# Transformer tower on one core: tokens reordered on the chip, the first tile of batch 0 normalised at the hand-over

## The reference

```python
h = _L0_tok_ref(x, log_dt, log_w_real, w_imag, 512)      # h: 8 batches, 256 tokens, 512 channels
h = h + _L0_attn_ref(_layernorm(h), w_q, w_k, w_v, w_o)  # 16 heads of 128, 4 kv heads, causal, window 256, rope
h = h + _L0_ffn_ref(_layernorm(h), ...)                  # gate by best of 8 experts, rank-8 update
...
def _L0_tok_ref(C, log_dt, log_w_real, w_imag, L):
    dt = exp(log_dt)                                     # 256 tokens ("H"), 64 poles each
    w = -exp(log_w_real) + 1j * w_imag
    dtA = w * dt[:, None]
    Cm = (C[..., 0] + 1j * C[..., 1]) * (exp(dtA) - 1.0) / w
    return 2 * einsum('chn,hnl->chl', Cm, exp(dtA[:, :, None] * arange(L))).real
```

## Time and profile before

| | |
|---|---|
| median of 3 runs | 824.38 us (823.27, 824.38, 827.25) |
| profiled execution, its own time | 827.14 us |
| its span | 825.0 us |
| TensorE busy | 755.7 us, 92% |
| VectorE, ScalarE, GpSimd busy | 569.8, 455.9, 441.6 us |
| mean granted clock | 0.976 |

### The profile page before, as it was taken

One profiled execution on the slowest core, in us unless ns is written; L12 is line 12 of the kernel. 1 busy time (PEld: TensorE's weight loads), 2 busy tenths in 40 slices (PEclk: granted clock), 3 DMA queues, 4 the chain that ended last, 5 costly groups with the idle time before them and its releaser, 6 DMA issues.

```text
span 825.0 us, 19690 instructions
## 1 busy us (share of the span) xinstructions
PE 755.7 (92%) x6964; PEld 685.9 (83%) x6964; DVE 569.8 (69%) x1605; ACT 455.9 (55%) x1249; POOL 441.6 (54%) x656
## 2 busy tenths in 40 slices
PE   0377878899999999999999999999999999999997
PEld 0176667799999999999999999999999999988973
DVE  7999747777776655666666655656655777778876
ACT  6634326555555656555556565555756555455432
POOL 0497825544444747444447474444656555565532
PEclk9998988899999999999999999999999999999997
DMA  9023360100010102000001020000010000000002
GB/s 210 0 60 68 79 230 27 39 1 0 0 39 1 52 2 77 0 0 0 0 1 52 1 79 0 0 0 0 14 40 1 2 1 27 26 25 0 26 14 90
DMA packets 30503, 26.47 MB, mean 32 GB/s; under 512 B 22446, under 2 KB 22830, under 8 KB 30198
## 3 DMA queue, kind: packets, MB, share of 16 engines
q1 hardware_dynamic: 30310, 25.77, 11.0%
q10 hardware_dynamic: 144, 0.07, 0.0%
HBM read 17.44 MB, written 8.39 MB: 31 GB/s over the span
## 4 chain that ended last, share of the span: by engine, by line
PE 80%; DVE 8%; POOL 6%; issue 3%; ACT 1%; DMA 1%; DVEq 0%; SPq 0%; POOLq 0%; ACTq 0%
PE bank_quad L1270 17%; PE bank_quad L1272 17%; PE bank_quad L1271 17%; PE bank_pair L1272 4%; PE bank_pair L1270 4%; PE bank_pair L1271 4%; POOL w_lo L433 2%; PE bank_pair L1425 2%; PE bank_quad L1282 2%; PE bank_quad L1365 2%; PE bank L1435 2%; PE bank_pair L1435 1%; PE bank L1439 1%; DVE bank_pair L936 1%; POOL kq_lo L503 1%
## 5 line engine op out<-in xcount | busy, mean ns | idle before, releaser
L1270 PE MATMUL bank_quad<-xt_hi,w_hi 128*128 (+1 forms) x768 | 217.1, 283 | 0.8 <-POOL w_lo L433 0.8
L1272 PE MATMUL bank_quad<-xt_lo,w_hi 128*128 (+1 forms) x768 | 214.8, 280 | 0.0
L1271 PE MATMUL bank_quad<-xt_hi,w_lo 128*128 (+1 forms) x768 | 214.8, 280 | 0.0
L1024 DVE TENSOR_TENSOR kq<-bank_quad,cst 128x512 f32<-128x512 f32 (+1 forms) x96 | 57.9, 603 | 141.1 <-ACT swap L697 106.5
L499 POOL TENSOR_TENSOR swap<-swap,cst 128x512 f32<-128x512 f32 (+1 forms) x96 | 105.7, 1103 | 82.5 <-ACT swap L697 79.7
L1270 PEld LDWEIGHTS bank_quad<-xt_hi,w_hi 128*128 128x128 f32 x768 | 144.9, 189 | 2.8 <-POOL w_lo L433 1.4
L1272 PEld LDWEIGHTS bank_quad<-xt_lo,w_hi 128*128 128x128 f32 x768 | 144.8, 189 | 0.0
L1271 PEld LDWEIGHTS bank_quad<-xt_hi,w_lo 128*128 128x128 f32 x768 | 144.5, 188 | 0.0
L357 POOL TENSOR_TENSOR spare<-cst 1x1 f32<-1x1 f32 x85 | 16.8, 197 | 213.9 <-DVE rinv L1164 139.9
L737 ACT ACTIVATE sm<-sm,mx 128x128 f32<-128x128 f32 (+1 forms) x256 | 113.6, 445 | 21.7 <-DVE mx L1152 21.6
L696 ACT ACTIVATE swap<-bank_quad 64x512 f32<-64x512 f32 (+1 forms) x96 | 50.2, 523 | 125.8 <-PE bank_quad L1272 123.2
(11 more groups left out here) (309 smaller groups left out, 1877.6 us busy)
## 6 DMA issues: line engine op xcount, KB each, us to landing
mixed<-st SPq DMA_DIRECT2D x32, 128.0 KB, 2.0
out<-x SPq DMA_DIRECT2D x16, 256.0 KB, 2.0
raw<-in_w_qkv SPq DMA_DIRECT2D x8, 384.0 KB, 3.7
raw<-in_w_o SPq DMA_DIRECT2D x10, 256.0 KB, 2.7
x<-mixed SPq DMA_DIRECT2D x2, 1280.0 KB, 10.3
norm_mem<-in_w_qkv SPq DMA_DIRECT2D x6, 384.0 KB, 3.9
x<-mixed SPq DMA_DIRECT2D x3, 512.0 KB, 4.9
norm_mem<-in_w_o SPq DMA_DIRECT2D x6, 256.0 KB, 2.8
```

The costliest lines, as they stand in the source:

```text
L1024: v.tensor_tensor(view(kq), src, table(cosT), ALU.mult).then_inc(kq_cos, 1)
L1270: mmul(dst, lh, rh, start=start and k == 0, stop=False, skip_group_check=True)
L1271: mmul(dst, ll, rh, start=False, stop=False, skip_group_check=True)
L1272: last = mmul(dst, lh, rl, start=False, stop=stop and k == n - 1, skip_group_check=True)
```

## The change

**Other tokens in each tile.** Tile 0 of `x` now holds tokens 0 to 63 and 128 to 191, tile 1 the others (`rows_of`). These 128 rows of tile 0 are what the first 8 chunks of the mixing make. The loads and the stores of the result follow that order. Transposes of the first norm write each tile's columns to their natural places (`columns_of`), so queries, keys and values stay in the natural order. The attention output comes out in natural order and is written by tile (`by_rows`), in runs of 64 columns; `ot_hi` and `ot_lo` have the tile as the outer dimension.

**Loads ahead.** When the first 8 chunks have landed, SyncE loads tile 0 of batch 0, and after each of the next seven stores tile 0 of one further batch. Behind the last store it loads tile 1 of batches 0, 1, 2, two chunks of `w_o`, and tile 1 of batches 3 to 7.

**Batch 0 in two halves.** Tile 0 of batch 0 is counted, normalised, transposed, rounded and split as soon as the engines have finished the mixing's tables and GpSimd its first `split_lo`; tile 1 follows when it has landed, with its transposes in banks 7 and 3. The dummy products are 2 ahead of the first transposes and 4 behind, in place of 7; the one behind the last transposes stays.

```diff
-        oth = sb("ot_hi", [P, QH, S], F32R)
-        otl = sb("ot_lo", [P, QH, S], F32R)
+        oth = sb("ot_hi", [P, TT, QH, P], F32R)
+        otl = sb("ot_lo", [P, TT, QH, P], F32R)
...
+        def rows_of(dram, t):
+            return dram.rearrange("(hh t p) d -> t hh p d", hh=2, t=TT)[t]
+        def columns_of(tile, t):
+            return tile.rearrange("p (hh t c) -> p t hh c", hh=2, t=TT)[:, t]
+        def columns_of_pair(tile, q, t):
+            return tile[:, 0, 2 * q:2 * q + 2, :].rearrange("p k (hh t c) -> p k t hh c", hh=2, t=TT)[:, :, t]
+        def pair_of(bank):
+            return banks[bank][:, 0:S].rearrange("p (k hh c) -> p k hh c", k=2, hh=2)
+        def by_rows(tile, j):
+            return tile[:].rearrange("p t h (hh c) -> p (h hh) t c", hh=2)[:, 4 * j:4 * j + 4]
+        def natural(bank):
+            return bank[:].rearrange("p (h t c) -> p h t c", t=TT, c=P // 2)
...
             rows = x_dram.rearrange("(hh q m t) c (a j) -> q hh (t c a) m j", hh=2, q=NQ, t=2, j=64)
-            with sp.Fori(0, NQ // 2) as it:
+            def store_mixed(q, s, evacuated):
+                sp.wait_ge(evac, evacuated)
+                for hh in range(2):
+                    sp.dma_start(rows[q, hh], st[s][:, hh, :, :]).then_inc(xd_out[s], 16)
+            def load_tokens(t, b, done):
+                sp.dma_start(x[:, t, b, :], rows_of(x_dram[:, b, :], t)).then_inc(done, 16)
+            with sp.Fori(0, NQ // 4) as it:
                 for s in range(2):
-                    sp.wait_ge(evac, it * 2 + (s + 1))
-                    for hh in range(2):
-                        sp.dma_start(rows[it * 2 + s, hh], st[s][:, hh, :, :]).then_inc(xd_out[s], 16)
+                    store_mixed(it * 2 + s, s, it * 2 + (s + 1))
+            for s in range(2):
+                sp.wait_ge(xd_out[s], 16 * 2 * (NQ // 4))
+            load_tokens(0, 0, x_early)
+            for b, done in ((1, x_second), (2, x_third), (3, x_rest), (4, x_rest), (5, x_rest), (6, x_rest), (7, x_rest)):
+                q = NQ // 2 + b - 1
+                store_mixed(q, q % 2, q + 1)
+                load_tokens(0, b, done)
+            store_mixed(NQ - 1, 1, NQ)
             for s in range(2):
                 sp.wait_ge(xd_out[s], 16 * 2 * (NQ // 2))
-            tokens_in = x_dram.rearrange("(t p) c d -> p t c d", t=TT)
-            sp.dma_start(x[:, :, 0, :], tokens_in[:, :, 0, :]).then_inc(x_first, 16)
-            sp.dma_start(x[:, :, 1, :], tokens_in[:, :, 1, :]).then_inc(x_second, 16)
-            sp.dma_start(x[:, :, 2, :], tokens_in[:, :, 2, :]).then_inc(x_third, 16)
+            load_tokens(1, 0, x_first)
+            load_tokens(1, 1, x_second)
+            load_tokens(1, 2, x_third)
             load_raw(KC)
             load_raw(KC + 1)
-            for t in range(TT):
-                sp.dma_start(x[:, t, 3:NB, :], tokens_in[:, t, 3:NB, :]).then_inc(x_rest, 16)
+            for b in range(3, NB):
+                load_tokens(1, b, x_rest)
...
-                    sp.dma_start(out[bb, t * P:(t + 1) * P, :], x[:, t, bb, :]).then_inc(stored, 16)
+                    sp.dma_start(rows_of(out[bb], t), x[:, t, bb, :]).then_inc(stored, 16)
...
             pool.wait_ge(pw_done, KC)
-            for n in range(KC):
+            def early_norm():
+                mv, rstd = norm_set(0)["mv"], norm_set(0)["rstd"]
+                wait_apart(pool, early_var, 1, 8)
+                nc.gpsimd.tensor_scalar(rstd[:, 0:1], mv[:, 0, 1:2], EPS, 1.0, ALU.add, ALU.mult).then_inc(early_pool, 1)
+                pool.wait_ge(early_pool, 1)
+                nc.gpsimd.tensor_tensor(rstd[:, 0:1], rstd[:, 0:1], cst[:, C_POW:C_POW + 1], ALU.pow).then_inc(early_rstd, 1)
+            split_lo(0)
+            early_norm()
+            for n in range(1, KC):
                 split_lo(n)
-            pool.wait_ge(x_first, 16)
+            def second_norm():
+                mv, rstd = norm_set(0)["mv"], norm_set(0)["rstd"]
+                wait_apart(pool, ln_var, 1, 8)
+                nc.gpsimd.tensor_scalar(rstd[:, 1:2], mv[:, 1, 1:2], EPS, 1.0, ALU.add, ALU.mult).then_inc(ln_pool, 1)
+                pool.wait_ge(ln_pool, 1)
+                nc.gpsimd.tensor_tensor(rstd[:, 1:2], rstd[:, 1:2], cst[:, C_POW:C_POW + 1], ALU.pow).then_inc(ln_rstd, 1)
...
+            def xt_half(q, t, bank):
+                return nc.scalar.activation(columns_of_pair(xt_h, q, t), pair_of(bank), ACT.Copy)
+            for q in range(2):
+                act.wait_ge(early_xt, q + 1)
+                xt_half(q, 0, 5 + q).then_inc(early_hi, 1)
...
-            xt1(0)
+            for q in range(2):
+                act.wait_ge(xt_ready, q + 1)
+                xt_half(q, 1, (7, 3)[q]).then_inc(xt_hi, 1)
...
-                    nc.scalar.activation(oth[:, 2 * j:2 * j + 2, :].rearrange("p h s -> p (h s)"),
-                                         banks[j][:], ACT.Copy).then_inc(ot_hi, 1)
+                    nc.scalar.activation(by_rows(oth, j), natural(banks[j]), ACT.Copy).then_inc(ot_hi, 1)
...
-            norm_stats(tokens(0), 0)
-            norm_apply(tokens(0), 0)
-            xt_rest(0)
-            dve.wait_ge(x_second, 16)
+            def half_apply(t):
+                mem = norm_set(0)
+                return v.tensor_scalar(mem["xn"][:, t, :], x[:, t, 0, :], mem["mv"][:, t, 0:1], mem["rstd"][:, t:t + 1],
+                                       ALU.subtract, ALU.mult)
+            def half_rest(q, t, bank):
+                return v.tensor_tensor(columns_of_pair(xt_l, q, t), pair_of(bank), columns_of_pair(xt_h, q, t).bitcast(F32),
+                                       ALU.subtract)
+            dve.wait_ge(x_early, 16)
+            norm_stat(tokens(0), 0)
+            wait_apart(dve, ln_st, 1, 4)
+            v.bn_aggr(norm_set(0)["mv"][:, 0, :], stats[:, 0, :]).then_inc(early_var, 1)
+            dve.wait_ge(early_rstd, 1)
+            half_apply(0).then_inc(early_xn, 1)
+            for q in range(2):
+                dve.wait_ge(early_hi, q + 1)
+                half_rest(q, 0, 5 + q).then_inc(early_lo, 1)
+            dve.wait_ge(x_first, 16)
+            norm_stat(tokens(0), 1)
+            wait_apart(dve, ln_st, 2, 4)
+            v.bn_aggr(norm_set(0)["mv"][:, 1, :], stats[:, 1, :]).then_inc(ln_var, 1)
+            dve.wait_ge(ln_rstd, 1)
+            half_apply(1).then_inc(xn_ready, 1)
+            for q in range(2):
+                dve.wait_ge(xt_hi, q + 1)
+                half_rest(q, 1, (7, 3)[q]).then_inc(xt_lo, 1)
+            dve.wait_ge(x_second, 32)
...
-                hs = slice(2 * j, 2 * j + 2)
-                v.tensor_tensor(otl[:, hs, :].rearrange("p h s -> p (h s)"), banks[j][:],
-                                oth[:, hs, :].rearrange("p h s -> p (h s)").bitcast(F32),
+                v.tensor_tensor(by_rows(otl, j), natural(banks[j]), by_rows(oth, j).bitcast(F32),
                                 ALU.subtract).then_inc(ot_lo, 1)
...
             pe.wait_ge(evac, NQ)
-            keep_warm(7)
-            def transpose_tokens(m, first_bank=5):
+            keep_warm(2)
+            def half_transposes(t, in_banks, done):
+                for q in range(2):
+                    for k in range(2):
+                        col = (2 * q + k) * P
+                        last = nc.tensor.transpose(banks[in_banks[q]][:, k * P:(k + 1) * P], xn[:, t, col:col + P], ident)
+                    last.then_inc(done, 1)
+            pe.wait_ge(early_xn, 1)
+            half_transposes(0, (5, 6), early_xt)
+            keep_warm(4)
...
+                            if natural:
+                                dst = columns_of(banks[first_bank + q][:, k * S:(k + 1) * S], t)
+                            else:
+                                dst = banks[first_bank + q][:, k * S + t * P:k * S + (t + 1) * P]
+                            last = nc.tensor.transpose(dst, normed[:, t, col:col + P], ident)
...
-                parts = [(oth[:, h, t * P:(t + 1) * P], otl[:, h, t * P:(t + 1) * P], woh[:, h, :], wol[:, h, :])
+                parts = [(oth[:, t, h, :], otl[:, t, h, :], woh[:, h, :], wol[:, h, :])
...
-            first_tokens(0)
+            pe.wait_ge(cw_done, 1)
+            pe.wait_ge(xn_ready, 1)
+            half_transposes(1, (7, 3), xt_ready)
             keep_warm(1)
             wait_split(pe, KC - 1)
+            pe.wait_ge(early_lo, 2)
             pe.wait_ge(xt_lo, 2)
             project(0, 0, True, lambda: None, lambda: first_tokens(1))
```

More of the change, by code:

```diff
@@ L327, in tower @@
         x_first, x_second, x_third, x_rest = sem("x_first"), sem("x_second"), sem("x_third"), sem("x_rest")
+        early_var, early_pool, early_rstd, early_xn, early_xt, early_hi, early_lo, x_early = (
+            sem("early_var"), sem("early_pool"), sem("early_rstd"), sem("early_xn"), sem("early_xt"), sem("early_hi"),
+            sem("early_lo"), sem("x_early"))
         pw_done, cw_mm, cw_done = sem("pw_done"), sem("cw_mm"), sem("cw_done")
@@ L355, in wait_apart @@
```

(32 more changed lines are left out.)

## The result

The kernel after took 887.79 us (median of 5 runs, 887.33 to 888.04), the kernel before 824.38 (5 runs): a ratio of 1.077, 95% interval 1.074 to 1.079. Slower by 63 us, where the prediction was 820.0 in 818.0 to 823.5.

A forecast was written before the change was run, and what follows sets the result against it. It took the chain of waits around the last mixed rows, with TensorE idle, as the bound there; projection start 3.75 us earlier plus 1.25 from the clock gave 5.0 us, forecast 820.0 us, range 818.0 to 823.5.

The forecast's parts named there:

- the margin of the mixing: SyncE's queue, second half's stores: 3.3 us spare per store against a 2.7 us load; 0.6 us margin even without overlap.
- Stores of the result keep their 2 KB rows: Result stores: row length unchanged, so no cost was taken.
- Rival 3: Mixing: loads hold up stores, ScalarE waits for its buffer; seven chunks at 1.4 us add 9.8, 829.8 us; chance 0.04.
- The load: Hand-over, second half of batch 0: 256 KB instead of 512, taking 2.7 us, landing at 104.9, 1.2 us earlier.
- Statistics of one tile: Hand-over, VectorE: one tile's statistics instead of two, 0.65 of 1.30 us.
- late next: Hand-over: GpSimd's remainders end at 106.3, after the variance's arrival at 105.95, so they set the second norm's start.
- One tile to normalise: Hand-over, VectorE: normalising one tile takes half of 1.01 us, so the first transpose comes at 108.25, 2.04 us earlier.
- The early half lies in the shadow of the last rows: Early tile's work between 97.7 and about 104.5 is hidden while last rows travel; uncovered, about 5 us.
- rival 1: Hand-over: TensorE's clock falls all the same, leaving a gain of 2.3 us, 822.7 us; chance 0.16.
- the dummy product would be hidden: Behind the last transposes: the remaining dummy product ends near 109.6 at full clock, hidden by the copies.
- The 1.25 us for the projection at full clock: Projection's start: if the clock stays up, its 2.5 us at half speed shrink by 1.25.
- Copies with runs of 64 columns: Attention output copies: at most some 10 ns each, taken as nothing; unhidden on 64 copies, 0.6 us.

The follow-up runs named there:

- e7: Kernel after with each tile's two blocks interleaved by partition (outermost dimension 64, one transfer per load or store), `ot_hi` and `ot_lo` copies in two: 820.98 us.
- e1: Kernel after with each token load and each result store issued as two transfers of 64 rows: 823.60 us, ratio to before 0.9997.
- e3: Kernel after with only the token loads split into two transfers of 64 rows: 843.86 us (one execution).
- e6: e1 with the second 64 rows of each of the last four result tiles issued on ScalarE's queue: 822.15 us, ratio to before 0.998.
- e5: e1 with six dummy products ahead of the last four transposes and none behind: 823.66 us, ratio to before 1.000.
- e8: e7 with the dummy products of e5: 820.64 us, ratio to before 0.996.
- e4: e1 without the early half of batch 0, token order and early loads kept: 826.66 us, ratio to before 1.003.

## Why the prediction was wrong

**The step that failed** is "The same size and the same 2 KB rows have a row: 2.7 us for the 256 KB loads of w_o", and with it "a 256 KB load takes 2.7" in the margin of the mixing and "Stores of the result keep their 2 KB rows", priced at nothing. I matched size and row length and left out the shape: the w_o load has an outer dimension that fills 16 engines, `rows_of` has 2. Alone such a transfer takes 5.1 us, not 2.7. It cost three times over: in the mixing and the hand-over 25.9 us, in step 0 and after it 10.6 by difference, at the end 24.5. The last of these was in none of my cases, because I had written the stores off by the length of their rows.

**Rival 3** named the right mechanism for the first part: loads hold up stores, ScalarE waits for its buffer. It decides over 5.3 us from a copy's end, I wrote; the buffer whose copies ended at 103.73 could be filled again at 115.20, 11.5 us after. The price of 1.4 us a chunk was 2.4 (16.5 over seven). The rival had no term for SyncE's own time either: behind piled-up two-engine loads an issue held it for 2 to 4 us, so even stores whose data were ready came late. Its chance of 0.04 rested on the wrong 2.7, and on a margin that was miscounted besides. Its "the margin is 0.6 us even if store and load never overlap" sets one load against a buffer's 6 us, but a store of 2.0 and a load of 2.7 come with every chunk, 3 us apart: without overlap they don't fit. In e7 they overlap, and the last pair of copies starts at 98.83, against 98.74 before. So it was overlap that saved the mixing there, not the margin.

**What was left of the forecast** is seen in e7, where the transfers are as I had priced them. Times are counted from the start of the last pair of `st` copies (98.74 in the earlier trace rows, 98.83 in e7).

- The load. I had the second half landed 6.2 us after that mark. Before it was 7.4, in e7 7.2. The forecast 1.2 us shrank to 0.2: the load took 3.3 us from its issue, not 2.7 (its kind's median is 3.4), and was issued 0.4 us later, as the last store took 2.7 us to land and not 2.0. This was the mis-sized term of the hand-over.
- Statistics of one tile: 0.69 us against 0.65, right.
- GpSimd as "late next": wrong. Its remainders ended 7.3 us after the mark, as I had worked out within 0.3, but the aggregate came at 8.1, so it stood idle for 0.87 us. In e7 these are the rows

```profile
102.38 3.78 POOL L471 TENSOR_TENSOR w_lo<-raw_more,w_hi 128x768 fp32r<-128x768 f32 x2
...
105.99 0.69 DVE L1043 BATCH_NORM_STATS2 stats<-x 128x6 f32<-128x512 f32 x1 [1.58 <-DMA x<-mixed]
...
107.03 0.18 POOL L382 TENSOR_TENSOR spare<-cst 1x1 f32<-1x1 f32 x1 [0.87 <-DVE norm L1118]
```

- One tile to normalise: 0.55 us in place of 1.01, right. The transposes came 10.0 us after the mark, forecast 9.5, before 11.55.
- The early half lies in the shadow of the last rows, right. Its normalisation took 2.02 us beside GpSimd's remainder of 1.80, and ended 0.3 us after it:

```profile
100.62 1.80 POOL L471 TENSOR_TENSOR w_lo<-raw,w_hi 128x768 fp32r<-128x768 f32 x1
100.69 2.02 DVE L1099 TENSOR_SCALAR norm_mem<-x,norm 128x512 f32<-128x512 f32 x1 [2.12 <-POOL norm L524]
```

  So it ended at 102.71, between the 102.3 that I had read from the earlier trace rows and the 103.1 by the rule in the Trainium skill's "SBUF — State Buffer" (section "SBUF: two separate sides"). The trace agrees with that rule in kind; nothing waited for it.
- The clock fell in e7 and e1 behind idle times of 1.99 and 2.15 us ahead of the last four transposes, and stayed at 1.00 in e3 and e6 behind 2.04 and 2.09. So rival 1 came true in two of these four profiles, against a chance of 0.16. I had said that the dummy product would be hidden; at half clock it ran until 110.99 in e1, 0.8 us past the operands of the product that followed. In e3 and e6 it was hidden. In e5 and e8, which have none behind the transposes, the clock stayed at 1.00.
- From the mark to the projection's second product: 15.35 before, 12.4 in e7, 11.7 in e8. That is 3.0 and 3.6 us, where I had 3.75. The 1.25 us for the projection at full clock don't show in full on top of that: from the mark to the first result store e7 wins 2.8 and e8 3.8 against the mean of six profiles, where the forecast was 5.0.
- Copies with runs of 64 columns cost nothing, right: `ot_hi` 597 ns before and after, `ot_lo` 678 and 677. In e7 they were two each, of 0.39 to 0.41 us, and still hidden: TensorE waited for them once, 0.5 us.
- The whole: e7 gains 2.8 us in the medians and e8 3.1, where the forecast was 4.4. With 16 engines, 820.98 and 820.64 us would have lain within the range. That is in part luck: the 4.4 was itself less than the sum of 5.0, and neither the load's 1.2 us nor, in e7, the clock came as the sum had them.

**What stays open** is why 64-row transfers from one queue move 205 GB/s at the share of busy time at which those of 128 rows move 322, and what decides whether the clock falls behind some 2 us of idle time. And the early half by itself wasn't timed with whole transfers. e1 and e4 ran on different chips; by their ratios to before (0.9997 and 1.0029) it is worth 2.6 us.

## What to carry to other kernels

Price a transfer by its pattern, not by its bytes and rows: look at the outermost dimension of both sides, and ask how many of 16 engines it fills. A rearrangement that put a 2 in front cost a factor of eight in engines here, and moving that dimension inward (p before hh) cost nothing but another order on the chip and copies in two parts. When a change adds transfers to a queue, give the issuing engine's time a term of its own, and when the kernel ends with a store, its landing is on the path in full. Where the median shows no gain, lay marks along the profile (first product, first store, last write, end) and take the time between marks, in every profile whose program is the same up to there: here one stretch won about 3 us and another gave back 2.8.

## What the runs showed of the hardware

- Result stores with an outermost dimension of 2, 4 and 16 kept 0.13, 0.26 and 0.95 of the DMA engines busy, and moved 51, 102 and 289 GB/s.
- An issue of SyncE took 0.34 us for 128 rows in one block and 0.5 to 0.6 for 64 rows, for 64 pairs or for 2 to 16 blocks, with nothing piled up; with two-engine transfers ahead of it, 2 to 5 us for most and 7.1 at most. Issues on ScalarE's queue took 0.5 to 0.6 (e6).
- Stores of 128 KB in 64 rows, all issued by SyncE, moved 205 GB/s where those of 256 KB in 128 rows moved 322. Issued half by SyncE and half by ScalarE, they moved 276 to 278.
- Ahead of the last four transposes the granted clock fell behind idle times of TensorE of 1.99 (e7) and 2.15 us (e1), and stayed at 1.00 behind 2.04 (e3), 2.09 (e6) and 0.47 (e5). Behind the 4.3 to 4.5 us of the three profiles of before it fell each time.
- A VectorE normalisation of 0.55 us alone took 2.02 beside a GpSimd subtraction of 1.80 that had started 0.07 us earlier (e7).
